# Expert routing rewritten: ranks row by row, counts and prefix on TensorE, the first two gathers issued inside the routing block

## The chip, the cores and the metric

The kernel runs on 1 core of one Trainium2 chip. The metric is device microseconds of one execution, the median of several. Lower is better.

## The reference, cut to what matters

A decoder layer on x (8, 256, 512): attention, then a long convolution with the context, then a mixture of experts, each on the layer-normalised x and added to it. The change is in the routing of the last one:

```python
logits = jnp.einsum('bsh,he->bse', x, Wr) + br          # 2048 tokens, E = 12 experts
probs = jax.nn.softmax(logits, axis=-1)
top_vals, top_idx = jax.lax.top_k(probs, K)             # K = 3
ew = jax.nn.softmax(top_vals, axis=-1)
for e in range(E):
    sel = top_idx == e
    mask = sel.any(axis=-1)
    cnt = sel.sum()
    w_e = jnp.sum(jnp.where(sel, ew, 0.0)) / jnp.maximum(cnt, 1)
    h = jax.nn.relu(jnp.einsum('bsh,hi->bsi', x, w1[e]) + b1[e])
    h = jnp.einsum('bsi,ih->bsh', h, w2[e]) + b2[e]
    out = out + mask[..., None] * (w_e * h)
```

An expert's weight w_e is one number for all its tokens. In `top_k` the lower index wins a tie.

## The kernel before, in words

The kernel is written for each engine by hand, in order, with semaphores. It has five blocks, one after the other: `attention`, `convolution`, `route`, `experts`, `finish`. At the end of a block all engines meet; the next block starts when the last has arrived.

`convolution` leaves the logits in `prob` (128 tokens on the partitions, NT = 16 token tiles, E = 12) and the normalised rows of x in DRAM, `xnd`.

`route` turns them into tables for `experts`. Tokens are sorted by expert into NTILE = 59 tiles of 128 places. `gidx` says which row of `xnd` a place gathers, `sidx` where its result is added, `wt` and `eid` are weight and expert of a tile, `tstart_i` is the first tile of an expert, `wexp` the weight of an expert. Almost all of it is one chain on VectorE (DVE); `do` means that the next instruction waits for this one. Its steps:

- softmax (L1193 to L1198), with an exp on ScalarE (ACT, L1147);
- rank of each expert of a token: all pairs are compared in one array of 16 x 12 x 12, greater (L1205), equal (L1206), equal and of a lower index (L1207), their sum (L1208), and the reduction over the rival (L1209); `sel` marks ranks under 3 (L1210);
- the softmax of the three best (L1212 to L1218), with a second exp on ACT;
- three fp32 matmuls (L1165 to L1167): places inside a token tile (`ps_c`), counts and weights by token tile (`ps_m`);
- a prefix sum over the 16 token tiles in five doubling steps (L1226 to L1231), the counts, the expert weights (L1236 to L1239);
- tiles by expert (L1242 to L1257), weight of each tile (L1258 to L1260), slot of each token and expert (L1262 to L1264), the slots of the three picks (L1266 to L1275);
- for each pick two one-hot tables in bf16, the place (16 x 128, L1286) and the tile with two values (16 x 59 each, L1284, L1288, L1289), that TensorE (PE) multiplies (L1174) into `ps_r`;
- `gidx` (L1300), `sidx` (L1304), the first expert's bias times its weight (L1306).

Beside it SP loads the weights of expert 0 in four quarters of 128 x 2560 (`w_lo`). ACT rounds each to fp32r (`upper`, L1151) and DVE takes the rest (`lower`, L1189), since a product is made of a high and a low part. ACT runs exp, `upper(0)`, exp, `upper(1)` to `upper(3)`. DVE runs `lower(0)` while it would wait for the counts and `lower(1)` while PE multiplies the last one-hot tables. `lower(2)` and `lower(3)` are the first work of DVE in `experts` (L1412), behind a wait for both copies of the gather indices (`gi_ready`, L1438).

`experts` starts with POOL (GpSimd): it copies an index column (L1438) and issues the indirect DMA that gathers 128 rows (`xg`, L1441), twice. PE transposes the first tile (`x_t`, L1564) when it has landed, ACT copies and rounds it (L1504, L1505), PE runs the first product (L1579, L1580 with `xh`, L1584 with `xl`, the low part that POOL makes, L1447), and from then on the tiles follow each other. The first product waits for the first two quarters of the weights, the second product (L1602) for all four. With all four split, SP starts to load the weights of expert 1, which DVE splits (L1405, L1407) and which must be there when the first tile of expert 1 comes; before each further expert DVE waits for PE (L1416).

Of the kernel before, what the change touches and what calls it, by code (L numbers as in the profile page):

```python
# [1081 lines left out]
def route(nc, cst, prob, w_hi, w_lo, split_done, wcat, b2, b2_sb, b2_in, b2_ready, tabs):  # L1082


    gidx, sidx, wt, eid, tstart_i, wexp = tabs
# [771 lines left out]
```

## Time and profile before

| | |
|---|---|
| median of 3 runs | 1593.04 us (1591.39 to 1593.26) |
| the profiled execution | 1590.1 us, its span 1588.1 us |
| PE busy | 1413.3 us (89%) |
| DVE busy | 792.1 us (50%) |
| POOL busy | 850.9 us (54%) |
| ACT busy | 679.8 us (43%) |
| granted TensorE clock, mean | 0.949 |

Times within the trace are in us from the start of the span. Busy shares are averages over five blocks with different limits; the routing block lies between about 545 and 601 us, where PE hardly works.

### The profile page before, as it was taken

What the parts mean: (1) busy time and instruction counts of PE and PEld (TensorE: products, weight loads), DVE (VectorE), ACT (ScalarE), POOL (GpSimd) and SP (SyncE); (2) the same over time, 40 slices, a digit from 0 to 9 for tenths busy, and PEclk for the clock granted to TensorE, in tenths of its full rate; (3) what the DMA queues carried; (4) which work ended last, traced back from release to release, by engine and by line L of the source; (5) the groups of instructions that cost most, each with busy time, mean ns of one, the idle gap of its engine ahead of it and who ended that gap; (6) DMA issues with size and microseconds to landing.
All of it is one profiled execution on the core that took longest, in us unless ns stands there. A gap on an engine that the chain in (4) does not pass through costs nothing. (4 is left out here: it accounts for less than half of the span.)

```text
span 1588.1 us, 27314 instructions
## 1 busy us (share of the span) xinstructions
PE 1413.3 (89%) x7642; PEld 1083.8 (68%) x7643; DVE 792.1 (50%) x1068; ACT 679.8 (43%) x1845; POOL 850.9 (54%) x990
## 2 busy tenths in 40 slices
PE   3899999669997417999999999999999999999956
PEld 1555555447775316888888888888888888888842
DVE  3456655548999698274434707446453552000003
ACT  0545546513444412444444444444444444444420
POOL 1444455134465204767666766767676766656530
PEclk9999999979999657999999999999999999999977
DMA  6000000034342514354444535444453542332115
GB/s 250 3 1 0 0 0 1 1 109 154 96 126 88 203 62 135 91 158 108 111 105 101 146 64 149 114 113 119 125 139 73 131 114 65 89 83 34 26 31 214
DMA packets 75461, 148.20 MB, mean 93 GB/s; under 512 B 9056, under 2 KB 13664, under 8 KB 74912
## 3 DMA queue, kind: packets, MB, share of 16 engines
q1 hardware_dynamic: 59424, 110.36, 22.3%
q0 software_dynamic: 14320, 35.40, 11.3%
q10 hardware_dynamic: 1680, 1.97, 0.4%
q8 instruction: 20, 0.33, 0.1%
q14 instruction: 17, 0.14, 0.0%
HBM read 115.11 MB, written 32.59 MB: 93 GB/s over the span
## 5 line engine op out<-in xcount | busy, mean ns | idle before, releaser
L1579 PE MATMUL ps_h<-w_hi,xh 128*128 x708 | 250.5, 365 | 1.5 <-ACT xh L1505 1.4
L1580 PE MATMUL ps_h<-w_lo,xh 128*128 x708 | 246.0, 359 | 0.0
L1602 PE MATMUL ps_y<-w_hi,hh 128*128 x590 | 239.9, 407 | 4.4 <-issue 4.4
L1407 DVE TENSOR_TENSOR w_lo<-stage,w_hi 128x512 f32 x220 | 223.9, 1018 | 27.0
L1603 PE MATMUL ps_y<-w_lo,hh 128*128 x590 | 233.8, 396 | 0.0
L1458 POOL TENSOR_TENSOR y<-y,b_sb 128x512 f32<-128x512 f32 x59 | 80.0, 1357 | 233.0 <-ACT y L1530 233.0
L1451 POOL TENSOR_TENSOR hl<-h,hh 128x1280 fp32r<-128x1280 f32 x59 | 190.9, 3235 | 13.1 <-ACT hh L1524 13.1
L933 PE MATMUL ps_b<-kv,toe 128*128 128x288 f32 x640 | 162.1, 414 | 12.9 <-DMA toe<-kpad 9.5
L1511 ACT ACTIVATE h<-ps_h 128x512 f32<-128x512 f32 x177 | 80.6, 528 | 212.8 <-POOL hl L1451 204.5
L1584 PE MATMUL ps_h<-w_hi,xl 128*128 x708 | 166.9, 357 | 0.0
L1520 ACT ACTIVATE h<-ps_td,b_now 128x128 f32<-128x128 f32 x590 | 158.6, 391 | 3.9 <-PE ps_td L1592 1.2
L1530 ACT ACTIVATE y<-ps_y,wt 128x512 f32<-128x512 f32 x59 | 40.7, 689 | 276.7 <-PE ps_y L1606 276.7
L933 PEld LDWEIGHTS ps_b<-kv,toe 128*128 128x128 f32 x640 | 123.0, 194 | 48.2 <-DMA toe<-kpad 10.4
L1579 PEld LDWEIGHTS ps_h<-w_hi,xh 128*128 128x128 f32 x708 | 133.4, 188 | 23.8 <-issue 2.1
L1580 PEld LDWEIGHTS ps_h<-w_lo,xh 128*128 128x128 f32 x708 | 133.7, 189 | 21.9
L1606 PE MATMUL ps_y<-w_hi,hl 128*128 x590 | 147.1, 395 | 0.0
L1405 DVE CAST w_hi<-stage 128x512 f32 x220 | 142.6, 648 | 5.7 <-DMA stage<-in_wcat 5.0
L1584 PEld LDWEIGHTS ps_h<-w_hi,xl 128*128 128x128 f32 x708 | 120.8, 188 | 21.8
L1602 PEld LDWEIGHTS ps_y<-w_hi,hh 128*128 128x128 f32 x590 | 111.8, 190 | 29.2 <-issue 4.6
L1416 DVE TENSOR_TENSOR turn<-wt 128x1 f32<-128x1 f32 x11 | 3.4, 312 | 253.4 <-PE ps_h L1584 253.4
L1606 PEld LDWEIGHTS ps_y<-w_hi,hl 128*128 128x128 f32 x590 | 110.5, 187 | 27.1
L1603 PEld LDWEIGHTS ps_y<-w_lo,hh 128*128 128x128 f32 x590 | 111.8, 190 | 24.3
(213 smaller groups left out, 2311.7 us busy)
## 6 DMA issues: line engine op xcount, KB each, us to landing
stage<-in_wcat SPq DMA_DIRECT2D x220, 256.0 KB
toe<-kpad SPq DMA_DIRECT2D x32, 256.0 KB, 3.3
cc<-in_ctx_rev SPq DMA_DIRECT2D x32, 192.0 KB, 3.4
w_lo<-in_wcat SPq DMA_DIRECT2D x4, 1280.0 KB, 11.8
acc<-added_c POOLq DMA_DIRECT2D x1, 4352.0 KB, 16.6
xs<-in_x SPq DMA_DIRECT2D x4, 1024.0 KB, 13.1
x2d<-xs SPq DMA_DIRECT2D x16, 256.0 KB, 2.5
xnd<-xn_c SPq DMA_DIRECT2D x16, 256.0 KB, 2.1
```

What stands on the lines that cost most here:

```text
L933: last = nc.tensor.matmul(view(ps[:], (4 * par + l) * 512, [[SPAN, B], [1, NPAIR]]), toe[:, par, (l - m) * P:(l - m + 1) * P], kv[:, buf, ...
L1405: nc.vector.tensor_copy(hi, stage[:, c % NSTAGE]).then_inc(w_rounded, 1)
L1407: nc.vector.tensor_tensor(lo, stage[:, c % NSTAGE], hi.bitcast(F32), ALU.subtract).then_inc(split_done, 1)
L1451: nc.gpsimd.tensor_tensor(hl[:], h[:], hh[:].bitcast(F32), ALU.subtract).then_inc(hl_ready, 1)
L1511: nc.scalar.activation(h[:, lo:hi], ps_h[:, c, 0:hi - lo], ACT.Copy).then_inc(h_evac, 1)
L1520: last = nc.scalar.activation(h[:, k * P:(k + 1) * P], ps_t[:, k // 4, (k % 4) * P:(k % 4 + 1) * P], ACT.Relu, bias=b1_now[:, k:k + 1])
L1579: nc.tensor.matmul(out, x_hi, part(w_hi, e, k * FF + lo, hi - lo), start=(k == 0), stop=False)
L1580: nc.tensor.matmul(out, x_hi, part(w_lo, e, k * FF + lo, hi - lo), start=False, stop=False)
L1584: last = nc.tensor.matmul(out, xl[:, k * P:(k + 1) * P], part(w_hi, e, k * FF + lo, hi - lo), start=False, stop=(k == KD - 1))
L1602: nc.tensor.matmul(ps_y[:], h_hi, part(w_hi, e, KD * FF + k * D, D), start=(k == 0), stop=False)
L1603: nc.tensor.matmul(ps_y[:], h_hi, part(w_lo, e, KD * FF + k * D, D), start=False, stop=False)
L1606: last = nc.tensor.matmul(ps_y[:], hl[:, k * P:(k + 1) * P], part(w_hi, e, KD * FF + k * D, D), start=False, stop=(k == KF - 1))
```

## The change

- Ranks: for each of the 12 experts its row is compared with the experts of lower index (>=) and with those of higher index (>), 22 instructions of 16 x 1 to 16 x 11 instead of four of 16 x 12 x 12. POOL clears the diagonal first. The reduction (L1237 of the changed kernel) stays.
- The largest probability is not searched again: it is the reciprocal of the softmax's sum, which is still in `den`. The subtraction for the second exp comes right behind the rank; `sel` is bf16 now.
- DVE sums `sel` and `ew` over the token tiles itself (`total`), so TensorE needs 12 columns for the counts and 12 for the weights. The places and the prefix over token tiles come from TensorE: 16 matmuls in bf16 that add up in `ps_c`. ACT makes the two bf16 matrices at the block's start, ahead of the first exp.
- `lower(0)` stands where `lower(1)` was; `lower(1)` stands behind `gidx`.
- The one-hot tables for tiles are 60 columns wide (59 used).
- POOL copies the first two index columns and issues the first two gathers inside `route`, as soon as `gidx` is there. The buffers `gi` and `xg` with their semaphores are made by the caller.
- The weights of the tiles and of the experts are made at the end, behind `lower(1)` and `sidx`.
- In `experts`, DVE waits for POOL's first `xl` instead of the index copies before it runs `lower(2)` and `lower(3)`.

```diff
--- before.py
+++ after.py
...
-def route(nc, cst, prob, w_hi, w_lo, split_done, wcat, b2, b2_sb, b2_in, b2_ready, tabs):
+def route(nc, cst, prob, w_hi, w_lo, split_done, wcat, b2, b2_sb, b2_in, b2_ready, xnd, first, tabs):
...
+    gi, xg, gi_ready, g_in = first
...
-        sel = sb("sel", [P, NT, E])
+        sel = sb("sel", [P, NT, E], BF16)
+        up_h = sb("up_h", [P, P], BF16)
+        one_h = sb("one_h", [P, P], BF16)
+        total = sb("total", [P, 2, E])
...
-        before = sb("before", [P, 2, NT + 1, E])
...
-        PLACE, TILE = NT * P, NT * NTILE
-        work = sb("work", [P, 2 * NT * E * E])
+        tile_f = sb("tile_f", [P, 4, NTILE])
+        COLS = NTILE + NTILE % 2
+        PLACE, TILE = NT * P, NT * COLS
+        work = sb("work", [P, max(NT * E * E, PLACE + 5 * TILE // 2)])
...
+            nc.scalar.activation(up_h[:], cst[:, C_UP:C_UP + P], ACT.Copy).then_inc(ones_ready, 1)
+            nc.scalar.activation(one_h[:], cst[:, C_ONE:C_ONE + P], ACT.Copy).then_inc(ones_ready, 1)
             exp(0)
             upper(0)
             exp(1)
             for q in range(1, NPART):
                 upper(q)
 
+        @block.gpsimd
+        def _(pool):
+            diag = view(work[:], 0, [[E * E, NT], [E + 1, E]])
+            nc.gpsimd.memset(diag, 0.0).then_inc(diag_zero, 1)
+            pool.wait_ge(gidx_ready, 1)
+            for i in range(2):
+                nc.gpsimd.tensor_copy(gi[:, i:i + 1], gidx[:, i:i + 1]).then_inc(gi_ready, 1)
+            pool.wait_ge(gi_ready, 2)
+            for i in range(2):
+                pool.indirect_dma_start(xg[:, i], None, xnd, bass.IndirectOffsetOnAxis(ap=gi[:, i:i + 1], axis=0))\
+                    .then_inc(g_in[i], 16)
+
         @block.tensor
         def _(pe):
 
+            ones = cst[:, C_ONE:C_ONE + P]
+            flat = sel[:].rearrange("p t e -> p (t e)")
+            pe.wait_ge(ones_ready, 2)
             pe.wait_ge(sel_ready, 1)
-            flat = sel[:].rearrange("p t e -> p (t e)")
-            nc.tensor.matmul(ps_c[:, 0:TE], cst[:, C_UP:C_UP + P], flat, start=True, stop=True)
-            nc.tensor.matmul(ps_m[:, 0:TE], cst[:, C_ONE:C_ONE + P], flat, start=True, stop=True)
-            nc.tensor.matmul(ps_m[:, TE:2 * TE], cst[:, C_ONE:C_ONE + P], ew[:].rearrange("p t e -> p (t e)"),
-                             start=True, stop=True).then_inc(counted, 1)
+            nc.tensor.matmul(ps_m[:, 0:E], ones, total[:, 0], start=True, stop=True).then_inc(counted, 1)
+            nc.tensor.matmul(ps_c[:, 0:TE], up_h[:], flat, start=True, stop=False)
+            for t in range(1, NT):
+                last = nc.tensor.matmul(ps_c[:, t * E:TE], one_h[:], flat[:, 0:TE - t * E], start=False,
+                                        stop=(t == NT - 1))
+            last.then_inc(placed, 1)
+            pe.wait_ge(ew_ready, 1)
+            nc.tensor.matmul(ps_w[:, 0:E], ones, total[:, 1], start=True, stop=True).then_inc(weighed, 1)
 
             for k in range(TOPK):
                 pe.wait_ge(hot_ready, k + 1)
                 oc, oa = place_hot(k), value_hot(k)
                 for t in range(NT):
-                    last = nc.tensor.matmul(ps_r[:, 0, 0:2 * NTILE], oc[:, t * P:(t + 1) * P],
-                                            oa[:, t * 2 * NTILE:(t + 1) * 2 * NTILE], start=(k == 0 and t == 0),
+                    last = nc.tensor.matmul(ps_r[:, 0, 0:2 * COLS], oc[:, t * P:(t + 1) * P],
+                                            oa[:, t * 2 * COLS:(t + 1) * 2 * COLS], start=(k == 0 and t == 0),
                                             stop=(k == TOPK - 1 and t == NT - 1))
                 last.then_inc(hot_used, 1)
...
-            gt = view(work[:], 0, [[E * E, NT], [E, E], [1, E]])
-            eq = view(work[:], NT * E * E, [[E * E, NT], [E, E], [1, E]])
-            other = view(prob[:], 0, [[E, NT], [0, E], [1, E]])
-            own = view(prob[:], 0, [[E, NT], [1, E], [0, E]])
-            low = view(cst[:], C_LOW, [[0, NT], [E, E], [1, E]])
-            v.tensor_tensor(gt, other, own, ALU.is_gt)
-            do(v.tensor_tensor(eq, other, own, ALU.is_equal))
-            do(v.tensor_tensor(eq, eq, low, ALU.mult))
-            do(v.tensor_tensor(gt, gt, eq, ALU.add))
-            do(v.tensor_reduce(rank[:], gt, AX_X, ALU.add))
+            dve.wait_ge(diag_zero, 1)
+            beats = view(work[:], 0, [[E * E, NT], [E, E], [1, E]])
+            for e in range(E):
+                own = view(prob[:], e, [[E, NT], [0, E - 1]])
+                for lo, hi, op in ((0, e, ALU.is_ge), (e + 1, E, ALU.is_gt)):
+                    if lo < hi:
+                        last = v.tensor_tensor(view(work[:], e * E + lo, [[E * E, NT], [1, hi - lo]]),
+                                               view(prob[:], lo, [[E, NT], [1, hi - lo]]),
+                                               view(prob[:], e, [[E, NT], [0, hi - lo]]), op)
+            do(last)
+            do(v.tensor_reduce(rank[:], beats, AX_X, ALU.add))
+            v.tensor_tensor(ex[:], prob[:], bc(den, E), ALU.subtract).then_inc(exp_in, 1)
             do(v.tensor_scalar(sel[:], rank[:], float(TOPK), None, ALU.is_lt))
-
-            do(v.tensor_reduce(mx, prob[:], AX_X, ALU.max))
-            v.tensor_tensor(ex[:], prob[:], bc(mx, E), ALU.subtract).then_inc(exp_in, 1)
+            v.tensor_reduce(total[:, 0], sel[:].rearrange("p t e -> p e t"), AX_X, ALU.add).then_inc(sel_ready, 1)
             dve.wait_ge(exp_out, 2)
-            do(v.tensor_tensor(ex[:], ex[:], sel[:], ALU.mult))
-            do(v.tensor_reduce(den, ex[:], AX_X, ALU.add))
-            do(v.reciprocal(den, den))
-            v.tensor_tensor(ew[:], ex[:], bc(den, E), ALU.mult).then_inc(sel_ready, 1)
-            v.memset(before[:, :, 0], 0.0)
+            do(v.scalar_tensor_tensor(ex[:], rank[:], float(TOPK), ex[:], ALU.is_lt, ALU.mult))
+            do(v.tensor_reduce(mx, ex[:], AX_X, ALU.add))
+            do(v.reciprocal(mx, mx))
+            do(v.tensor_tensor(ew[:], ex[:], bc(mx, E), ALU.mult))
+            v.tensor_reduce(total[:, 1], ew[:].rearrange("p t e -> p e t"), AX_X, ALU.add).then_inc(ew_ready, 1)
             v.tensor_copy(iota_h[:], cst[:, C_IOTA:C_IOTA + P])
-            lower(0)
             dve.wait_ge(counted, 1)
 
 
             count, inv, weight, ntile, tstart, tend = (wexp[:] if i == 2 else cnt[:, i] for i in range(6))
-            do(v.tensor_copy(before[:, 0, 1:], ps_m[:, 0:TE].rearrange("p (t e) -> p t e", e=E)))
-            step, par = 1, 0
-            while step <= NT:
-                if step > 1:
-                    v.tensor_copy(before[:, 1 - par, 1:step], before[:, par, 1:step])
-                do(v.tensor_tensor(before[:, 1 - par, step:], before[:, par, step:], before[:, par, 0:NT + 1 - step],
-                                   ALU.add))
-                step, par = 2 * step, 1 - par
-            upto = before[:, par]
-            do(v.tensor_copy(count, upto[:, NT]))
-            v.tensor_reduce(weight, view(ps_m[:], TE, [[1, E], [E, NT]]), AX_X, ALU.add)
-            do(v.tensor_scalar(inv, count, 1.0, None, ALU.max))
-            do(v.reciprocal(inv, inv))
-            do(v.tensor_tensor(weight, weight, inv, ALU.mult))
-
+            do(v.tensor_copy(count, ps_m[:, 0:E]))
...
+            v.tensor_scalar(inv, tstart, float(P), None, ALU.mult)
...
-            do(v.tensor_tensor(tile_e, view(cst[:], C_IOTA, [[0, NTILE], [1, E]]), bc(expert, E), ALU.is_equal))
-            do(v.tensor_tensor(tile_e, tile_e, view(weight, 0, [[0, NTILE], [1, E]]), ALU.mult))
-            do(v.tensor_reduce(wt[:], tile_e, AX_X, ALU.add))
-
-            do(v.tensor_tensor(slot[:], upto[:, 0:NT], ps_c[:, 0:TE].rearrange("p (t e) -> p t e", e=E), ALU.add))
-            do(v.tensor_scalar(inv, tstart, float(P), None, ALU.mult))
-            do(v.tensor_tensor(slot[:], slot[:], view(inv, 0, [[0, NT], [1, E]]), ALU.add))
+
+            dve.wait_ge(placed, 1)
+            do(v.tensor_tensor(slot[:], ps_c[:, 0:TE].rearrange("p (t e) -> p t e", e=E),
+                               view(inv, 0, [[0, NT], [1, E]]), ALU.add))
...
-                do(v.tensor_tensor(in_tile, view(iota_h[:], 0, [[0, NT], [1, NTILE]]),
-                                   bc(h_tile[:, k * NT:(k + 1) * NT], NTILE), ALU.is_equal))
+                do(v.tensor_tensor(in_tile, view(iota_h[:], 0, [[0, NT], [1, COLS]]),
+                                   bc(h_tile[:, k * NT:(k + 1) * NT], COLS), ALU.is_equal))
                 v.tensor_tensor(oc, view(iota_h[:], 0, [[0, NT], [1, P]]),
                                 bc(h_place[:, k * NT:(k + 1) * NT], P), ALU.is_equal)
                 v.tensor_scalar(oa[:, :, 0], in_tile, cst[:, C_TOK:C_TOK + 1], None, ALU.mult)
-                v.tensor_tensor(oa[:, :, 1], in_tile, bc(iota_h[:, 0:NT], NTILE), ALU.mult).then_inc(hot_ready, 1)
-            lower(1)
+                v.tensor_tensor(oa[:, :, 1], in_tile, bc(iota_h[:, 0:NT], COLS), ALU.mult).then_inc(hot_ready, 1)
+            lower(0)
...
+            m_place, m_tile = ps_r[:, 0, 0:NTILE], ps_r[:, 0, COLS:COLS + NTILE]
+            used, tok, to = (tile_f[:, i] for i in range(1, 4))
...
-            v.tensor_copy(gidx[:], tok)
-            do(v.tensor_scalar(expert, tok, trash, None, ALU.subtract))
-            do(v.tensor_tensor(expert, expert, used, ALU.mult))
-            do(v.tensor_scalar(expert, expert, trash, None, ALU.add))
-            v.tensor_copy(sidx[:], expert)
+            v.tensor_copy(gidx[:], tok).then_inc(gidx_ready, 1)
+            dve.wait_ge(gi_ready, 2)
+            lower(1)
+            do(v.tensor_scalar(to, tok, trash, None, ALU.subtract))
+            do(v.tensor_tensor(to, to, used, ALU.mult))
+            do(v.tensor_scalar(to, to, trash, None, ALU.add))
+            v.tensor_copy(sidx[:], to)
+
+            dve.wait_ge(weighed, 1)
+            v.tensor_copy(weight, ps_w[:, 0:E])
+            do(v.tensor_scalar(inv, count, 1.0, None, ALU.max))
+            do(v.reciprocal(inv, inv))
+            do(v.tensor_tensor(weight, weight, inv, ALU.mult))
+            tile_w = view(work[:], 0, [[E, NTILE], [1, E]])
+            do(v.tensor_tensor(tile_w, view(cst[:], C_IOTA, [[0, NTILE], [1, E]]), bc(expert, E), ALU.is_equal))
+            do(v.tensor_tensor(tile_w, tile_w, view(weight, 0, [[0, NTILE], [1, E]]), ALU.mult))
+            do(v.tensor_reduce(wt[:], tile_w, AX_X, ALU.add))
             dve.wait_ge(b2_in, 16)
             v.tensor_scalar(b2_sb[:, 0], b2_sb[:, 0], wexp[:, 0:1], None, ALU.mult).then_inc(b2_ready, 1)
...
+    gi, xg, gi_ready, g_in = first
...
-        gi = sb("gi", [P, 2], U32)
...
-        xg = sb("xg", [P, 2, D])
...
-            dve.wait_ge(gi_ready, 2)
+            dve.wait_ge(xl_ready, 2)
...
-            gather(0, 0)
-            gather(1, 1)
...
+                    first = (right("gi", [P, 2], U32), right("xg", [P, 2, D]), busy.enter_context(nc.semaphore("gi_ready")),
+                             [busy.enter_context(nc.semaphore(f"g_in{i}")) for i in range(2)])
```

The order of the ranks on DVE. Before (`work` holds all pairs, `rank` the result):

```order
L1198 TENSOR_TENSOR prob<-ex,col 128x192
L1205 TENSOR_TENSOR work<-prob 128x2304
L1206 TENSOR_TENSOR work<-prob 128x2304
L1207 TENSOR_TENSOR work<-work,cst 128x2304
L1208 TENSOR_TENSOR work<-work 128x2304
L1209 TENSOR_REDUCE rank<-work 128x192
L1210 TENSOR_SCALAR sel<-rank 128x192
L1212 TENSOR_REDUCE col<-prob 128x16
L1213 TENSOR_TENSOR ex<-prob,col 128x192
```

and of the change, the first and the last of the 22 comparisons with what follows:

```order
L1225 TENSOR_TENSOR prob<-ex,col 128x192
L1233 TENSOR_TENSOR work<-prob 128x16x11
...
L1233 TENSOR_TENSOR work<-prob 128x16x11
L1237 TENSOR_REDUCE rank<-work 128x192
L1238 TENSOR_TENSOR ex<-prob,col 128x192
L1239 TENSOR_SCALAR sel<-rank 128x192
L1240 TENSOR_REDUCE total<-sel 128x12
L1242 SCALAR_TENSOR_TENSOR ex<-rank,ex 128x192
```

The four large operations became 22 small ones, and the input of the second exp (`ex`) is made before `sel`.

The end of the routing on DVE, from `gidx` on. Before:

```order
L1300 CAST gidx<-tile_f 128x59
L1301 TENSOR_SCALAR tile_f<-tile_f,cst 128x59
L1302 TENSOR_TENSOR tile_f<-tile_f 128x59
L1303 TENSOR_SCALAR tile_f<-tile_f,cst 128x59
L1304 CAST sidx<-tile_f 128x59
L1306 TENSOR_SCALAR b_sb<-b_sb,wexp 128x512
```

and of the change:

```order
L1310 CAST gidx<-tile_f 128x59
L1216 TENSOR_TENSOR w_lo<-w_lo,w_hi 128x2560
L1313 TENSOR_SCALAR tile_f<-tile_f,cst 128x59
L1314 TENSOR_TENSOR tile_f<-tile_f 128x59
L1315 TENSOR_SCALAR tile_f<-tile_f,cst 128x59
L1316 CAST sidx<-tile_f 128x59
L1319 COPY wexp<-ps_w 128x12
L1320 TENSOR_SCALAR cnt<-cnt 128x12
L1321 RECIPROCAL cnt<-cnt 128x12
L1322 TENSOR_TENSOR wexp<-wexp,cnt 128x12
L1324 TENSOR_TENSOR work<-cst,tile_f 128x708
L1325 TENSOR_TENSOR work<-work,wexp 128x708
```

A quarter of the weights (`w_lo`) and the weights of experts and tiles now stand between `gidx` and the end of the block.

POOL, at the border of `route` and `experts`. Before, all of it in `experts`:

```order
L1427 UNCONDITIONAL_BRANCH
L1438 COPY gi<-gidx 128x1
L1435 TENSOR_TENSOR tick<-wt 128x1
L1441 DMA xg<-xnd,gi 128x512
L1438 COPY gi<-gidx 128x1
L1435 TENSOR_TENSOR tick<-wt 128x1
L1441 DMA xg<-xnd,gi 128x512
L1447 TENSOR_TENSOR xl<-xf,xh 128x512
```

and of the change, where the two branches after the gathers are the way into `experts`:

```order
L1169 UNCONDITIONAL_BRANCH
L1172 MEMSET work 128x16x12
L1175 COPY gi<-gidx 128x1 x2
L1178 DMA xg<-xnd,gi 128x512 x2
L1087 UNCONDITIONAL_BRANCH
L1447 UNCONDITIONAL_BRANCH
L1467 TENSOR_TENSOR xl<-xf,xh 128x512
```

Copies and gathers moved in front of the block's end.

## Rows read from the trace of the kernel before

**Rows 1.** Busy time of each engine by stretch (start:end, length, engines, clock, DMA share, GB/s).

```profile
566.00:602.00 36.00, 5.49 (x49) 4.53 (x48) 33.58 (x67) 3.10 (x2) 0.25 (x2) 0.50 0.00 0
640.00:740.00 100.00, 100.00 (x519) 83.92 (x518) 43.69 (x55) 45.59 (x113) 69.84 (x79) 1.00 0.44 108
```

**Rows 2.** Timeline of PE (start, length, operation, idle before it and its releaser).

```profile
606.03 1.12 PE L1564 MATMUL ps_xd<-cst,xg 128*128 128x128 f32 x4 [8.11 <-DMA xg<-xnd,gi]
608.60 0.79 PE L1579 MATMUL ps_h<-w_hi,xh 128*128 x1 [1.44 <-ACT xh L1505]
```

**Rows 3.** Timeline of DVE, the comparisons of the ranks.

```profile
548.15 2.56 DVE L1205 TENSOR_TENSOR work<-prob 128x2304 f32<-128x2304 f32 x1
550.62 2.55 DVE L1206 TENSOR_TENSOR work<-prob 128x2304 f32<-128x2304 f32 x1
...
558.39 2.55 DVE L1209 TENSOR_REDUCE rank<-work 128x192 f32<-128x2304 f32 x1
```

**Rows 4.** Timeline of ACT in the routing: the first quarter rounded, the second exp.

```profile
554.18 2.34 ACT L1151 ACTIVATE w_hi<-w_lo 128x2560 fp32r<-128x2560 f32 x1 [7.13 <-DMA w_lo<-in_wcat]
562.06 0.36 ACT L1147 ACTIVATE ex<-ex 128x192 f32<-128x192 f32 x1 [5.54 <-DVE ex L1213]
```

**Rows 5.** Timeline of DVE, second softmax, first quarter, prefix, weights, slots.

```profile
562.45 0.36 DVE L1215 TENSOR_TENSOR ex<-ex,sel 128x192 f32<-128x192 f32 x1 [0.43 <-ACT ex L1147]
...
563.94 2.82 DVE L1189 TENSOR_TENSOR w_lo<-w_lo,w_hi 128x2560 fp32r<-128x2560 f32 x1
566.68 0.35 DVE L1226 COPY before<-ps_m 128x192 f32<-128x192 f32 x1
...
570.28 0.17 DVE L1242 TENSOR_SCALAR cnt<-cnt 128x12 f32<-128x12 f32 x1
...
574.40 0.88 DVE L1258 TENSOR_TENSOR work<-cst,tile_f 128x708 f32<-128x708 f32 x1
...
577.17 0.35 DVE L1262 TENSOR_TENSOR slot<-before,ps_c 128x192 f32<-128x192 f32 x1
...
578.16 0.36 DVE L1266 SCALAR_TENSOR_TENSOR ex<-rank,slot 128x192 f32<-128x192 f32 x1
```

**Rows 6.** Timeline of DVE, the one-hot tables and the second quarter.

```profile
581.35 1.14 DVE L1284 TENSOR_TENSOR work<-iota_h,slot_h 128x944 bf16<-128x944 bf16 x1
582.53 2.29 DVE L1286 TENSOR_TENSOR work<-iota_h,slot_h 128x2048 bf16<-128x2048 bf16 x1
...
596.03 2.82 DVE L1189 TENSOR_TENSOR w_lo<-w_lo,w_hi 128x2560 fp32r<-128x2560 f32 x1
```

**Rows 7.** Timeline of DVE, the end of the routing and the start of the experts.

```profile
599.62 0.19 DVE L1300 CAST gidx<-tile_f 128x59 uint32<-128x59 f32 x1
...
600.65 0.48 DVE L1306 TENSOR_SCALAR b_sb<-b_sb,wexp 128x512 f32<-128x512 f32 x1
603.95 5.58 DVE L1412 TENSOR_TENSOR w_lo<-w_lo,w_hi 128x2560 fp32r<-128x2560 f32 x2 [2.82 <-POOL gi L1438]
```

**Rows 8.** Timeline of POOL from the start of the experts.

```profile
601.67 0.18 POOL L1438 COPY gi<-gidx 128x1 uint32<-128x1 uint32 x1 [61.82 <-POOLq L1086]
...
604.27 3.40 POOL L1441 DMA_INDIRECT xg<-xnd,gi  x1
608.35 2.32 POOL L1447 TENSOR_TENSOR xl<-xf,xh 128x512 fp32r<-128x512 f32 x1 [0.68 <-ACT xh L1505]
```

**Rows 9.** The line of the gathers: length of one in ns (min/median/max), and time to landing.

```profile
L1441 POOL DMA_INDIRECT xg<-xnd,gi x59: 992/1037/3400, 602.5 to 1482.3; - x59
...
DMA to landing us min/median/max: 3.3/3.8/6.4
```

**Rows 10.** Timeline of DVE, its first wait for PE before an expert's weights.

```profile
673.55 0.16 DVE L1416 TENSOR_TENSOR turn<-wt 128x1 f32<-128x1 f32 x1 [27.09 <-PE ps_h L1584]
```

**Rows 11.** Busy time by stretch at the start of the experts.

```profile
608.00:613.00 5.00, 4.41 (x11) 3.50 (x12) 3.11 (x3) 0.27 (x1) 3.63 (x4) 0.52 0.60 182
613.00:618.00 5.00, 5.00 (x31) 4.29 (x29) 3.71 (x8) 1.42 (x3) 0.00 (x0) 1.00 0.70 240
```

More of the change, by code:

```diff
@@ L1115, in route @@
         ps_m = psum("ps_m", [P, 512])
+        ps_w = psum("ps_w", [P, 512])
         ps_r = psum("ps_r2", [P, 1, 512])
@@ L1118, in route @@
         exp_in, exp_out = sem("exp_in"), sem("exp_out")
-        sel_ready, counted = sem("sel_ready"), sem("counted")
+        ones_ready, sel_ready, counted, placed = sem("ones_ready"), sem("sel_ready"), sem("counted"), sem("placed")
+        ew_ready, weighed = sem("ew_ready"), sem("weighed")
+        diag_zero, gidx_ready, step_g = sem("diag_zero"), sem("gidx_ready"), sem("step_g")
         hot_ready, hot_used = sem("hot_ready"), sem("hot_used")
@@ L1248, in _ @@
             v.tensor_copy(tstart_i[:], tstart[0:1])
+            v.tensor_scalar(inv, tstart, float(P), None, ALU.mult)
             do(v.tensor_tensor(tend, tstart, ntile, ALU.add))
             tile_e = view(work[:], 0, [[E, NTILE], [1, E]])
-            expert, is_e, first = tile_f[:, 0], tile_f[:, 1], tile_f[:, 2]
+            expert = tile_f[:, 0]
             do(v.tensor_tensor(tile_e, view(cst[:], C_IOTA, [[1, NTILE], [0, E]]), view(tend, 0, [[0, NTILE], [1, E]]),
@@ L1288, in _ @@
                 v.tensor_scalar(oa[:, :, 0], in_tile, cst[:, C_TOK:C_TOK + 1], None, ALU.mult)
-                v.tensor_tensor(oa[:, :, 1], in_tile, bc(iota_h[:, 0:NT], NTILE), ALU.mult).then_inc(hot_ready, 1)
-            lower(1)
+                v.tensor_tensor(oa[:, :, 1], in_tile, bc(iota_h[:, 0:NT], COLS), ALU.mult).then_inc(hot_ready, 1)
+            lower(0)
             dve.wait_ge(hot_used, TOPK)
-            m_place, m_tile = ps_r[:, 0, 0:NTILE], ps_r[:, 0, NTILE:2 * NTILE]
-            used, tok = is_e, first
+            m_place, m_tile = ps_r[:, 0, 0:NTILE], ps_r[:, 0, COLS:COLS + NTILE]
+            used, tok, to = (tile_f[:, i] for i in range(1, 4))
             trash = cst[:, C_TRASH:C_TRASH + 1]
@@ L1309, in experts @@
 def experts(nc, cst, w_hi, w_lo, stage, stage_in, split_done, wcat, b2, b2_sb, b2_in, b2_ready, b1_sb, xnd, x2d, x2,
-            x2_in, acc, tabs):
+            x2_in, acc, first, tabs):
     gidx, sidx, wt, eid, tstart_i, wexp = tabs
+    gi, xg, gi_ready, g_in = first
     with ExitStack() as ctx:
@@ L1344, in experts @@
         CHUNKS = [(0, 512), (512, 1024), (1024, FF)]
-        gi_ready, si_ready = sem("gi_ready"), sem("si_ready")
-        g_in = [sem("g_in0"), sem("g_in1")]
+        si_ready = sem("si_ready")
         x_done = sem("x_done")
@@ L1795, in decoder_layer @@
                     b2_ready = busy.enter_context(nc.semaphore("b2_ready"))
+                    first = (right("gi", [P, 2], U32), right("xg", [P, 2, D]), busy.enter_context(nc.semaphore("gi_ready")),
+                             [busy.enter_context(nc.semaphore(f"g_in{i}")) for i in range(2)])
                     route(nc, cst, prob, w_hi, w_lo, split_done, a["wcat"], a["L0_ffn_b2"], b2_sb,
-                          b2_in, b2_ready, tabs)
+                          b2_in, b2_ready, xnd, first, tabs)
                     experts(nc, cst, w_hi, w_lo, stage, stage_in, split_done, a["wcat"], a["L0_ffn_b2"], b2_sb, b2_in,
-                            b2_ready, b1_sb, xnd, x2d, x2, x2_in, acc, tabs)
+                            b2_ready, b1_sb, xnd, x2d, x2, x2_in, acc, first, tabs)
                 finish(nc, cst, x2, x2_in, acc, a["L0_ffn_Wp1"], a["L0_ffn_bp1"], a["L0_ffn_Wp2"], a["L0_ffn_bp2"], out)
```

1 line of the change is left out of this document (removed).

## The prediction, made before the changed kernel ran

> **What bounds the kernel now.** I read the busy time by stretch first. Between 640 and 740 us PE is busy all the time at full clock, and it stays so until the last tiles; between 566 and 602 it is busy for 5.5 us of 36 while DVE is for 33.6 [rows 1]. So the experts are bound by PE and the routing by DVE. The timeline of PE shows the border: the first transposition starts at 606.03, released by the landing of the gather, and the first product at 608.60 [rows 2]. From there PE is hardly idle. Whatever brings 608.60 forward comes off the whole time one to one, if nothing new holds PE afterwards. So I follow the DVE chain through the routing, then the way from its end to the first product.
>
> **The chain on DVE up to gidx.** Prices first. The same kind of operation takes 2.56 us for 2304 elements [rows 3] and about 0.88 for 708 [rows 5]: about 1.04 ns an element and a fixed part near 0.16. Started without a wait the next one begins 2.47 after the first (548.15 to 550.62), which is 0.07 over its elements; with a wait, 944 elements take 1.18 to the next start (581.35 to 582.53 [rows 6]), 0.20 over them.
>
> (a) Ranks. Removed: 548.15 to 558.39, 10.24 us [rows 3]. Added: 22 comparisons of 16 x 1 to 16 x 11, 2 x 16 x 66 = 2112 elements, 2.2 us, and 22 fixed parts. Only the last is waited for, so I take 0.07 each, 1.5 us: 3.7 in all. The ends are 2.2 (no fixed part) and 22 x 0.20 + 2.2 = 6.6 (each as if waited for). The reduction (2.55, and a few hundredths to the next start) then starts at 551.9 instead of 558.39 and the rank is there at 554.5. POOL's clearing of the diagonal starts with the block, two microseconds ahead of its use, and costs nothing.
>
> (b) The second exp does not keep up. ex is ready at 554.5 + 0.36 = 554.9. But ACT has upper(0) before exp(1) in its order, and upper(0) starts at 554.18, when its quarter has landed, and takes 2.34 [rows 4]. So exp starts at 556.5, and DVE goes on 0.4 behind that, as before (562.06 to 562.45 [rows 4, 5]), at 556.9 instead of 562.45. DVE, done with sel and total at about 555.4, has waited 1.5 us by then: **-5.6** for (a) and (b). This also caps (a): up to 1.5 us of extra cost in the ranks is hidden by that wait, beyond it it counts. The two bf16 copies that ACT makes lie before its first exp, while DVE makes that one's input; they may cost 0 to 0.3, I take 0.
>
> (c) From there to the old start of lower(0), 1.49 us before (562.45 to 563.94 [rows 5]); now one reduction more (0.27) and a wait: **+0.3**.
>
> (d) lower(0) leaves this place, 563.94 to 566.68 [rows 5]: **-2.7**. It takes the place of lower(1) at 596.03 [rows 6], with the same length and the same cover for PE's last product. What lower(0) covered, the wait for the counts, is short now: one matmul of 12 columns, 3 us ahead of its use.
>
> (e) Prefix, counts, expert weights: 566.68 to 570.28 [rows 5], 3.6 us, become one copy of 0.2: **-3.4**. The 16 prefix matmuls are needed some 6 us after their input; the three 192-column fp32 ones before fit in the 2.8 us of lower(0). Hidden.
>
> (f) Tile weights leave: 574.40 to 577.17 [rows 5], **-2.8**.
>
> (g) Slots: 577.17 to 578.16 becomes one operation of 0.39 and one unwaited one of 0.08: **-0.5**.
>
> (h) One-hot tables: 581.35 to 596.03 [rows 6], 14.7 us. 60 instead of 59 columns add 16 elements to each of nine operations, 0.15 us, and the tensor_scalar may gain as much: 0. The 2048-element comparison in bf16 takes 2.29, one element a cycle like fp32 [rows 6], although its rows are of even width: one operand repeats one value along the row, as in the tile tables.
>
> Sum: gidx starts **14.7** earlier, at 584.9 instead of 599.62 [rows 7].
>
> **From gidx to the first product.** (i) DVE now waits for POOL's two copies (0.18 each [rows 8]) with a semaphore each way: +0.6; bounds 0.4 and 2.8, what DVE waited for the copies at 603.95 when an issue lay between them [rows 7]. Then lower(1) +2.7, expert weights +0.8, tile weights +2.7. The routing ends on DVE at 601.13 (600.65 + 0.48 [rows 7]) - 14.7 + 6.8 = 593.2, that is **-7.9**.
>
> (j) Before, 4.90 us passed from DVE's end to the first transposition: 0.54 to the first instruction of POOL (601.67 [rows 8]), then copy, issue, landing. Now the gather is issued at about 585.9. It takes 3.8 us to land in the median and 6.4 at most [rows 9], so it is there by 592.3, before the block ends. What is left is the entry into the block: 0.54 is the nearest row; I take 0.6 for PE, between 0.5 and 2.0, since PE's own entry is hidden behind the gather in this trace. **-4.3**. The steps from there to the first product (2.57 us [rows 2]) stay.
>
> (k) lower(2) and lower(3), 5.6 us [rows 7], now start behind xl, about 6 us later against the product. The second product that needs them comes 18 us after the first. Expert 1's weights are also loaded 6 us later against PE; DVE had 27.1 us to spare before the next expert [rows 10]. Price 0 unless that cover is gone. In exchange xl is no longer slowed by them; it was not waited for.
>
> (l) The clock: 0.52 of full between 608 and 613, 1.00 after [rows 11], so it rose about 4 us behind the first product. I take the same; a rise at once gives 2 us (half of 4), one that comes twice as late costs 2.
>
> **Sum:** -7.9 - 4.3 = **-12.2 us**. The profiled execution took 1590.1, which gives 1577.9. It lies 2.9 under the median of the runs (1593.04), so for the median I say **1580.8**. The unknowns (a, at most +1.4 beyond the cover; i and j, -0.3 to +3.6; l, 2 either way; not all at once) make this case's own range 1578 to 1584.5.
>
> A rule against the change: the Trainium skill (VectorE: DVE Perf Modes, The TRN2 errata) says small instructions pay a fixed cost each, (N + 151) cycles at 0.96 GHz for an fp32 tensor_tensor. By it the 22 comparisons would be an estimated 5.7 us, 2.0 more than I take, 0.5 beyond the cover, and the time 1581.3; the length of a single operation agrees [rows 3], but the start of the next one does not wait for it.
>
> **Rivals.**
> 1. *The entry replaces the gather.* PE has its own first instructions to do in the block and nothing in the trace shows their length; if the start of the block is as long as the old wait, (j) gives nothing: 1585.1. For: POOL is the only engine seen entering there. Against: it needed 0.54 only [rows 8]. 8%.
> 2. *DVE holds up POOL.* The issue that ran beside lower(2) took 3.40 against 1.04 in the median [rows 8, 9], and xl 2.32. Now both issues stand beside lower(1) and the tile weights. Two of 3.4 end at 592.9, just inside; if the second lasts until DVE is done and then takes its 1.0, the block ends 1 to 2 us late: 1582 to 1583. 8%. The Trainium skill (GPSIMD Engine Reference, 8. Key points) says that GpSimd contends with Vector instructions of two SBUF inputs; the rows agree.
> 3. *The even width pays.* If the tile tables ran at two elements a cycle, six operations of 1.14 would save half a microsecond each: 1577.9. Against: the 128-wide one does not [rows 6]. 3%. The Trainium skill (VectorE: DVE Perf Modes, What auto-detection actually checks) asks for 16-bit operands of step 1, which the repeated operand is not.
> 4. *Slower: the clock stays low.* PE idles longer between the last one-hot product and the transposition (about 10.5 us against 8.1 [rows 2]). If TensorE then stayed at 1.2 GHz, each microsecond costs half of one. To lose the 12.2 and come out 3.2 slower it would have to stay low for about 31 us longer than the 4 us of now. Against: once PE was busy without a gap it rose at once [rows 11]. 1.5%, 1597 or more.
>
> **How the numbers follow.** The forecast has 78%, the rivals 8, 8, 3 and 1.5; 1.5 remain for a loss that just cancels the gain. 0.2% is 3.2 us, about what a measurement of this kernel can tell from no change. Faster by more than that (under 1589.9) are all but the last two: 0.97; 0.015 and 0.015 for the rest. The range from 1577.5 to 1585.5 holds the first case, rival 1, 2 and 3.
>
> **What would show it.** Right: the rank's reduction starts about 3.7 us after prob; DVE then waits about 1.5 us for ACT's exp behind upper(0); no rows of the prefix on DVE; gidx near 585; POOL's gathers in the routing, the first longer than 1.04; the first transposition near 594 with no DMA in front, and the first product near 596.4; the second expert's first wait of DVE still over 15 us. Wrong: comparisons that each cost 0.2 over their elements; a transposition that waits for the gather or for the entry; a clock that rises much later; any PE wait for weights behind the first tiles.

## The result, and the profile after

| | before | after |
|---|---|---|
| median | 1592.65 us (4 runs, 1591.39 to 1593.26) | 1563.72 us (4 runs, 1563.44 to 1566.66) |
| ratio | | 0.9824, 95% interval 0.9807 to 0.9841 |
| profiled execution | 1590.1 us, span 1588.1 | 1563.66 us, span 1561.5 |
| routing's first DVE instruction to first product | 62.70 us | 50.94 us |
| first product to first matmul of `finish` | 940.6 us | 924.05 us |

28.9 us came off, where 12.2 were forecast; the range ended at 1577.5. The last two rows of the table say where: the forecast is about the first, and that one fell by 11.8. Another 16.6 us came off the experts, where the forecast had put nothing. Both are differences between the starts of instructions: 545.90 (DVE, L1193) to 608.60 [rows 2] to 1549.24 before

```profile
1549.24 9.80 PE L1705 MATMUL ps_pool<-o_sb,cst 128*4 128x512 f32 x16 [14.22 <-DMA o_sb<-acc]
```

and in the timeline of the changed kernel (DVE and PE):

```profile
548.38 0.35 DVE L1220 TENSOR_REDUCE col<-prob 128x16 f32<-128x192 f32 x1 [0.56 <-PEq L660]
...
596.78 1.09 PE L1582 MATMUL ps_xd<-cst,xg 128*128 128x128 f32 x4 [10.79 <-ACTq L1515]
599.32 0.79 PE L1597 MATMUL ps_h<-w_hi,xh 128*128 x1 [1.44 <-ACT xh L1523]
...
1523.37 6.90 PE L1723 MATMUL ps_pool<-o_sb,cst 128*4 128x512 f32 x11 [14.28 <-DMA o_sb<-acc]
```

The first transposition waits for no DMA any more. The routing began 2.5 us later in this execution than in the one of before; over all runs of this study it began between 545.8 and 550.1, in old and new kernels alike, so this is the variation of the blocks ahead of it.

The routing itself, DVE's timeline of the changed kernel, against [rows 3, 5, 6, 7]:

```profile
550.61 3.82 DVE L1233 TENSOR_TENSOR work<-prob 128x176 f32<-128x176 f32 x22
554.47 2.55 DVE L1237 TENSOR_REDUCE rank<-work 128x192 f32<-128x2304 f32 x1
557.06 0.36 DVE L1238 TENSOR_TENSOR ex<-prob,col 128x192 f32<-128x192 f32 x1
557.33 0.25 DVE L1239 TENSOR_SCALAR sel<-rank 128x192 bf16<-128x192 f32 x1
557.62 0.51 DVE L1240 TENSOR_REDUCE total<-sel 128x12 f32<-128x192 bf16 x1
559.33 0.36 DVE L1242 SCALAR_TENSOR_TENSOR ex<-rank,ex 128x192 f32<-128x192 f32 x1 [1.20 <-ACT ex L1154]
...
561.33 0.16 DVE L1252 COPY cnt<-ps_m 128x12 f32<-128x12 f32 x1
561.52 0.17 DVE L1254 TENSOR_SCALAR cnt<-cnt 128x12 f32<-128x12 f32 x1
...
569.29 1.16 DVE L1294 TENSOR_TENSOR work<-iota_h,slot_h 128x960 bf16<-128x960 bf16 x1
...
584.07 2.82 DVE L1216 TENSOR_TENSOR w_lo<-w_lo,w_hi 128x2560 fp32r<-128x2560 f32 x1
...
587.66 0.19 DVE L1310 CAST gidx<-tile_f 128x59 uint32<-128x59 f32 x1
588.31 2.83 DVE L1216 TENSOR_TENSOR w_lo<-w_lo,w_hi 128x2560 fp32r<-128x2560 f32 x1 [0.46 <-POOL gi L1175]
...
595.51 0.49 DVE L1328 TENSOR_SCALAR b_sb<-b_sb,wexp 128x512 f32<-128x512 f32 x1
```

22 comparisons in 3.86 us; a new wait of 1.20 for ACT's exp; one-hot tables of the same 14.8 us; gidx 39.28 us after the first instruction instead of 53.72.

The experts. The busy time by stretch has 500 us of PE at 100% and full clock in both kernels. First the kernel before, then the changed one (columns as in [rows 1]):

```profile
740.00:1240.00 500.00, 500.00 (x2574) 418.83 (x2573) 245.51 (x316) 230.63 (x576) 339.18 (x384) 1.00 0.46 115
```

```profile
740.00:1240.00 500.00, 500.00 (x2614) 424.69 (x2613) 253.19 (x324) 236.92 (x594) 352.09 (x395) 1.00 0.47 117
```

Same clock, same busy share, but 1.6% more matmuls. The transpositions of x, one group per tile, give the period of a tile. Before, 15.54 us, then after, 15.28:

```profile
704.44 0.60 PE L1564 MATMUL ps_xd<-cst,xg 128*128 128x128 f32 x4
719.98 0.60 PE L1564 MATMUL ps_xd<-cst,xg 128*128 128x128 f32 x4
```

```profile
708.49 0.60 PE L1582 MATMUL ps_xd<-cst,xg 128*128 128x128 f32 x4
723.77 0.60 PE L1582 MATMUL ps_xd<-cst,xg 128*128 128x128 f32 x4
```

Over 48 tiles the period is 15.540 and 15.287 us. 0.253 us times 59 tiles is 14.9 of the 16.6. All instructions of a tile are the same in both kernels. What the diff does change there is one thing that I had read past: `gi` (8 bytes per partition) and `xg` (4096) left the left side of SBUF, and all buffers behind them moved down. In the built programs xh, xl, hh and hl, the stationary operands of the products (the ones that PE loads ahead of a matmul), start at a multiple of 64 bytes before and 32 beyond one after; the weights, the moving operands that stream through, start 32 beyond one in both.

### The profile page after: what moved, and what is told of

Read it like the earlier page. It is cut to its first block and busy times, and to the rows that moved or that the text cites. A ratio compares the mean times of both kernels' runs of the same rounds, so it can differ in the third digit from the quotient of the medians.

```text
span 1561.5 us, 27353 instructions
## 1 busy us (share of the span) xinstructions
PE 1396.8 (89%) x7656; PEld 1080.8 (69%) x7657; DVE 783.9 (50%) x1075; ACT 680.7 (44%) x1847; POOL 862.8 (55%) x989
## 5 line engine op out<-in xcount | busy, mean ns | idle before, releaser
L1427 DVE TENSOR_TENSOR w_lo<-stage,w_hi 128x512 f32 x220 | 236.3, 1074 | 27.0
L1597 PE MATMUL ps_h<-w_hi,xh 128*128 x708 | 247.1, 361 | 1.5 <-ACT xh L1523 1.4
L1598 PE MATMUL ps_h<-w_lo,xh 128*128 x708 | 242.2, 354 | 0.0
L1425 DVE CAST w_hi<-stage 128x512 f32 x220 | 134.3, 610 | 6.5 <-DMA stage<-in_wcat 6.0
## 6 DMA issues: line engine op xcount, KB each, us to landing
xs<-in_x SPq DMA_DIRECT2D x4, 1024.0 KB, 13.7
```

Of the source, the lines that this page charges most:

```text
L1425: nc.vector.tensor_copy(hi, stage[:, c % NSTAGE]).then_inc(w_rounded, 1)
L1427: nc.vector.tensor_tensor(lo, stage[:, c % NSTAGE], hi.bitcast(F32), ALU.subtract).then_inc(split_done, 1)
L1597: nc.tensor.matmul(out, x_hi, part(w_hi, e, k * FF + lo, hi - lo), start=(k == 0), stop=False)
L1598: nc.tensor.matmul(out, x_hi, part(w_lo, e, k * FF + lo, hi - lo), start=False, stop=False)
```

## The experiments

The first six move buffers by unused bytes and leave every instruction as it is.

**The old kernel with 32 bytes ahead of the experts' buffers.**

```diff
+        pad = sb("pad", [P, 8])
         gi = sb("gi", [P, 2], U32)
```

> The kernel before, with one unused buffer of 32 bytes per partition ahead of the first buffer of the experts block, so that all buffers there (xh, xl, hh, hl, which PE loads as stationary operands, among them) start 32 bytes later: at 32 beyond a multiple of 64, as in the changed kernel, instead of at a multiple of 64. The routing is the old one. Theory A (the start address of the buffers that PE loads decides how far apart matmuls start): tile period 15.54 -> about 15.29 us, time about 1592.7 - 15 = 1577.5. Theory B (the experts block got faster through what the change does in the routing, or through the 4 KB of xg that left the left side): no change, 1592.7, period 15.54.

Measured 1576.87 us (1575.8 to 1579.02, ratio to before 0.9898, interval 0.9881 to 0.9914), period 15.287:

```profile
706.89 0.60 PE L1565 MATMUL ps_xd<-cst,xg 128*128 128x128 f32 x4
722.18 0.60 PE L1565 MATMUL ps_xd<-cst,xg 128*128 128x128 f32 x4
```

The routing is the old one (62.79 us to the first product), and 15.9 us are gone. Theory B falls: neither the routing nor the 4 KB of xg, which are still on the left here, made the experts faster.

**The same with 64 bytes.**

```diff
+        pad = sb("pad", [P, 16])
         gi = sb("gi", [P, 2], U32)
```

> The kernel before with 64 unused bytes in the same place: all buffers of the experts block move, but stay at multiples of 64. Theory A: no change, 1592.7 and a period of 15.54. Rival A2 (not the alignment, but any move of the buffers against each other or against the weights changes it): some other period than 15.54.

1591.21 us (1590.08 to 1594.79, ratio 0.9994, interval 0.9984 to 1.0003), period 15.533. Moving alone does nothing.

**The changed kernel with 32 bytes**, so that its buffers start at multiples of 64 again.

```diff
+        pad = sb("pad", [P, 8])
         si = sb("si", [P, 2], U32)
```

> The changed kernel with 32 unused bytes ahead of the buffers of the experts block, so that they start at multiples of 64 again. Theory A: the period goes back to about 15.54 and the time to about 1563.7 + 15 = 1579; what is left of the gain, some 12 to 14 us, is the routing's. Theory B: 1563.7, period 15.29.

1579.07 us (1577.41 to 1579.59, ratio 0.9906), period 15.540:

```profile
711.14 0.60 PE L1583 MATMUL ps_xd<-cst,xg 128*128 128x128 f32 x4
726.68 0.60 PE L1583 MATMUL ps_xd<-cst,xg 128*128 128x128 f32 x4
```

This is the change without its side effect: 13.7 us faster than before by the medians, 11.6 by the stretch of the routing (51.14 against 62.70). Of the 2 us between them 1.2 lie in the clock of the last tile, see (l) below.

**The changed kernel with the weights moved by 32 bytes instead.**

```diff
+                pad_r = late.enter_context(nc.sbuf_tensor("pad_r", [P, 8], F32, side="right"))
                 w_hi = late.enter_context(nc.sbuf_tensor("w_hi", [P, 2, WS], F32R, side="right"))
```

> The changed kernel with 32 unused bytes beyond the weights, so that w_hi and w_lo (the moving operands) start at a multiple of 64 and xh, xl, hh, hl stay at 32 beyond one. Theory A1 (the stationary operand's own start decides): period 15.29, 1563.7. Theory A3 (stationary and moving operand must start alike within 64 bytes): period about 15.54, time about 1579. If the moving operand's own start at a multiple of 64 is good by itself, the period falls under 15.29.

1578.08 us (1577.06 to 1579.29, ratio 0.9906), period 15.540:

```profile
708.81 0.60 PE L1582 MATMUL ps_xd<-cst,xg 128*128 128x128 f32 x4
724.35 0.60 PE L1582 MATMUL ps_xd<-cst,xg 128*128 128x128 f32 x4
```

The stationary operands are where the fast kernel has them, and it is slow. It is not their own start that counts. The buffers behind the weights on that side (`stage`, `xg`, `gi`) move by 32 bytes too, but do not explain it: `xg` starts 32 beyond a multiple of 64 in the fast first experiment as well, and all of them start in the next run, which is fast, where they start here.

**Both moved**, weights and stationary operands at multiples of 64.

```diff
+        pad = sb("pad", [P, 8])
         si = sb("si", [P, 2], U32)
...
+                pad_r = late.enter_context(nc.sbuf_tensor("pad_r", [P, 8], F32, side="right"))
                 w_hi = late.enter_context(nc.sbuf_tensor("w_hi", [P, 2, WS], F32R, side="right"))
```

> The changed kernel with both moves: the weights start at a multiple of 64 and so do xh, xl, hh, hl. Stationary and moving operand start alike again, at 0 instead of at 32. Theory A3 (alike within 64 bytes is what counts): period 15.29, time 1563.7. Theory A4 (each operand costs by itself when it starts at a multiple of 64, and only 32 beyond is good): a period of 15.54 or more, 1579 or more.

1565.89 us (1565.64 to 1568.08, ratio 0.9839, interval 0.9824 to 0.9854), period 15.283:

```profile
709.66 0.60 PE L1583 MATMUL ps_xd<-cst,xg 128*128 128x128 f32 x4
724.95 0.60 PE L1583 MATMUL ps_xd<-cst,xg 128*128 128x128 f32 x4
```

Fast again, at other addresses: theory A3 holds and A4 falls.

**Only the operands of the second product moved**, the changed kernel with the 32 bytes between xl and h. Behind them h, hh, hl and y move.

```diff
         xl = sb("xl", [P, KD * P], F32R)
+        pad = sb("pad", [P, 8])
         h = sb("h", [P, FF])
```

> The changed kernel with 32 unused bytes between xl and h: xh and xl still start like the weights (32 beyond a multiple of 64), hh and hl, the stationary operands of the second product, no longer do. Theory A3 for each matmul by itself: the 30 matmuls of the second product lie about 233 ns apart again, those of the first product stay at about 229, the period becomes 15.29 + 30 x 0.0045 = 15.42, the time 1563.7 + 8 = 1571.5. Rival (the whole block changes its pace by something else that moves with the buffers): 15.29 or 15.54.

1571.44 us (1570.52 to 1571.98, ratio 0.9868), period 15.411. The groups by line show it product by product. The changed kernel, first the `xl` matmuls of the first product, then the `hl` ones of the second (between the bars busy us and mean ns of one, behind them the idle time ahead):

```profile
L1602 PE MATMUL ps_h<-w_hi,xl 128*128 x708 | 164.1, 354 | 0.0
L1624 PE MATMUL ps_y<-w_hi,hl 128*128 x590 | 144.9, 392 | 0.0
```

this kernel:

```profile
L1603 PE MATMUL ps_h<-w_hi,xl 128*128 x708 | 164.7, 355 | 0.0
L1625 PE MATMUL ps_y<-w_hi,hl 128*128 x590 | 147.1, 395 | 0.0
```

and the changed one with all of them moved (the third experiment):

```profile
L1603 PE MATMUL ps_h<-w_hi,xl 128*128 x708 | 167.5, 358 | 0.0
L1625 PE MATMUL ps_y<-w_hi,hl 128*128 x590 | 147.1, 395 | 0.0
```

The first product keeps its pace (355), the second has the slow one (395). So the price is paid in the product whose own operands start unlike, and not by the block as a whole.

The other runs take the routing apart, on the changed kernel.

**The first two gathers back in the experts block.**

```diff
-            pool.wait_ge(gidx_ready, 1)
-            for i in range(2):
-                nc.gpsimd.tensor_copy(gi[:, i:i + 1], gidx[:, i:i + 1]).then_inc(gi_ready, 1)
-            pool.wait_ge(gi_ready, 2)
-            for i in range(2):
-                pool.indirect_dma_start(xg[:, i], None, xnd, bass.IndirectOffsetOnAxis(ap=gi[:, i:i + 1], axis=0))\
-                    .then_inc(g_in[i], 16)
...
-            dve.wait_ge(gi_ready, 2)
             lower(1)
...
+            gather(0, 0)
+            gather(1, 1)
             x_lo(0)
```

> The changed kernel with the first two gathers (index copies and indirect DMAs) back at the start of the experts block; all buffers and the rest of the routing as changed. Theory: the landing of the first gather is on the path again, 1.27 -> about 5.4 us from the routing's last DVE instruction to the first transposition, and DVE is spared 0.5 us of waiting for the index copies: first product 3.6 us later, about 1567.3. Rival (the block's entry alone costs as much, or the reordering of DVE's work did it): less than 1 us.

1568.70 us (1567.83 to 1571.25), 5.0 over the changed kernel by the medians and 3.3 by the stretch from the routing to the first product (54.26 against 50.94), where 3.6 were expected; the other 1.7 us are not placed. The timeline at the border:

```profile
594.98 0.49 DVE L1320 TENSOR_SCALAR b_sb<-b_sb,wexp 128x512 f32<-128x512 f32 x1
596.00 0.18 POOL L1450 COPY gi<-gidx 128x1 uint32<-128x1 uint32 x1 [47.00 <-POOLq L1087]
...
600.30 1.11 PE L1576 MATMUL ps_xd<-cst,xg 128*128 128x128 f32 x4 [14.30 <-DMA xg<-xnd,gi]
```

From DVE's end (595.47) to the transposition 4.83 us, as before the change; the landing is on the path again.

**The second exp ahead of the first rounding.**

```diff
             exp(0)
-            upper(0)
             exp(1)
+            upper(0)
```

> The changed kernel with ACT's second exp ahead of the rounding of the first quarter of the weights. Theory: DVE's 1.20 us wait for that exp goes, everything behind it comes 1.2 us sooner, about 1562.5; the rounding of the first quarter comes 0 to 1 us later and is still 20 us ahead of its use. Rival (something else is late there, such as the counts from TensorE): no gain.

1561.32 us (1560.36 to 1564.98), 1.1 less in the traces (49.84 against 50.94). DVE's wait is gone:

```profile
555.10 0.50 DVE L1240 TENSOR_REDUCE total<-sel 128x12 f32<-128x192 bf16 x1
555.51 0.35 DVE L1242 SCALAR_TENSOR_TENSOR ex<-rank,ex 128x192 f32<-128x192 f32 x1
```

**The old comparisons.** The four large instructions of the kernel before in place of the 22, the rest as changed.

```diff
-            beats = view(work[:], 0, [[E * E, NT], [E, E], [1, E]])
-            for e in range(E):
...
-            do(v.tensor_reduce(rank[:], beats, AX_X, ALU.add))
+            gt = view(work[:], 0, [[E * E, NT], [E, E], [1, E]])
...
+            v.tensor_tensor(gt, other, own, ALU.is_gt)
+            do(v.tensor_tensor(eq, other, own, ALU.is_equal))
+            do(v.tensor_tensor(eq, eq, low, ALU.mult))
+            do(v.tensor_tensor(gt, gt, eq, ALU.add))
+            do(v.tensor_reduce(rank[:], gt, AX_X, ALU.add))
```

> The changed kernel with the four large comparisons of the old one for the ranks (and without the cleared diagonal). They take 10.2 us instead of 3.86, but the 1.2 us that DVE waits for the second exp go: theory 5.2 us slower, about 1568.9. If the wait behind the rounding did not cover anything, it would be 6.4.

1568.81 us (1567.1 to 1570.01), 5.1 slower; 5.2 in the traces (56.16). With the ranks late, DVE found the exp ready. The wait behind the rounding had hidden 1.2 of the 6.4 us that the small comparisons save.

**The changed kernel and the one with the early exp, side by side.**

> The changed kernel as it is, on the same chip as the next one: 1563.7.

> The changed kernel with ACT's second exp ahead of the first rounding, once more, beside the changed kernel on the same chip: 1.1 us faster by the stretch from routing to first product in the traces (49.83 against 50.94), 1562.6. If the 2.4 us between the medians of the first look were real, 1561.3.

1563.42 us (5 runs, 1563.15 to 1565.65; ratio to before 0.9823, interval 0.981 to 0.9837) and 1561.10 us (5 runs, 1559.15 to 1567.09; 0.9812, interval 0.9793 to 0.9831). The intervals overlap. The traces have 51.15 and 49.85 us for the stretch that the edit touches, so I take 1.1 to 1.3 us as its worth, and this kernel as the best of the study; the medians alone would not carry that.

## Why the prediction was wrong, point by point

What failed is a term that was put at nothing without a reason: the pace of the tiles. Behind "Whatever brings 608.60 forward comes off the whole time one to one" the sum has nothing for the experts but (k) and (l), both at 0. I took the block for unchanged because its instructions are, and did not follow where its buffers went. The missing term is 14.9 us by the period of the tiles; the run that gives it alone measured 15.9. The order of the instructions and the trace of before could not have priced it. But that two buffers of 8 and 4096 bytes leave from ahead of the stationary operands of the bound engine stands in the diff (in the built programs these operands move by 4128 bytes, not a multiple of 64), and a bound of either sign for it would have been due.

The kernel without that effect (1579.07) lies 1.7 under the forecast of 1580.8 and inside its own range. That it lies under it is luck: its stretch from the routing to the first product fell by 11.6, less than the 12.2 of the sum, and the clock of the last tile gave 1.2 that the sum had not seen. The steps of the sum, in the changed kernel:

- **(a) Ranks.** Forecast 3.7 for 2112 elements in 22 instructions, measured 3.86: the price of 0.07 us for an instruction that nobody waits for holds down to 16 elements (0.10 us from start to start; 0.26 with 176). The Trainium skill's formula (VectorE: DVE Perf Modes, The TRN2 errata) gave an estimated 5.7; no run here shows it for a chain without waits.
- **(b) ACT's order.** DVE resumed 10.95 us after its first instruction instead of 16.55, -5.6 as forecast. The wait was 1.20 instead of 1.5, since summing sel took 0.51. The early-exp run showed the wait real and the old comparisons showed its cover.
- **(c)** +0.5 instead of +0.3, for the second such sum. **(e)** 0.19, as forecast. **(h)** 14.78 against 14.68: the wider tables bring nothing, rival 3 is out. gidx -14.4 instead of -14.7.
- **(i)** The wait for the index copies cost 0.46; DVE's end came 8.34 after gidx, +6.8 against before, as forecast.
- **(j)** From DVE's end at 596.00 to the transposition 0.78 us, forecast 0.6: -4.1 instead of -4.3. Rival 1 is out. Rival 2's mechanism is there and its price is not. POOL's timeline, the two gathers:

```profile
588.51 3.64 POOL L1178 DMA_INDIRECT xg<-xnd,gi  x1 [0.29 <-POOL gi L1175]
592.46 0.95 POOL L1178 DMA_INDIRECT xg<-xnd,gi  x1 [0.31 <-issue]
```

  and what the trace says of that line's landings:

```profile
DMA to landing us min/median/max: 3.5/4.8/6.1
```

  The first issue lasted 3.64 us beside lower(1), and landed after 6.1 at most, 594.6. The second took 0.95 us beside the tile weights, and POOL was done at 593.4. PE began at 596.78, so 2.2 us of cover are left. The Trainium skill's rule (GPSIMD Engine Reference, 8. Key points), contention with DVE instructions of two SBUF inputs, fits the first issue and xl, which took 1.27 instead of 2.32 [rows 8] with DVE idle. The second issue does not show it: it was as short as one alone, though a comparison of 708 elements with two such inputs (L1324, 592.73 to 593.63) ran beside it.
- **(k)** DVE had 18.6 us to spare at the first wait, where it was 27.1 [rows 10]:

```profile
662.83 0.25 DVE L1436 TENSOR_TENSOR turn<-wt 128x1 f32<-128x1 f32 x1 [18.61 <-PE ps_h L1602]
```

  The cover held, at two thirds of its size.
- **(l)** In this execution the clock rose sooner, not later (busy time by stretch, the granted clock third from the end):

```profile
599.00:602.00 3.00, 2.68 (x6) 2.15 (x7) 1.54 (x1) 0.00 (x0) 2.84 (x3) 0.50 0.00 0
602.00:607.00 5.00, 5.00 (x25) 4.16 (x24) 4.08 (x3) 1.03 (x2) 4.74 (x2) 0.96 0.00 0
```

  That is some 3 us behind the first product instead of 4, worth half a microsecond. It is not the change: in the second trace of the same kernel (`e10_after_again`) the first product started at 597.29, and the clock was back only some 5.7 us behind it:

```profile
597.00:602.00 5.00, 4.71 (x11) 3.75 (x12) 3.58 (x2) 0.00 (x0) 4.72 (x4) 0.50 0.01 3
602.00:607.00 5.00, 5.00 (x27) 4.26 (x27) 2.05 (x2) 1.20 (x2) 2.85 (x1) 0.90 0.34 96
```

  Over all traces of this study it was 3.0 to 6.0 us. Rival 4, the slower one, needed 31 us more and is out. With 14.9 for the period and 0.5 here, about 1.2 us of the experts' 16.6 are left. They lie in the last tile, for which the sum had no term. There PE is idle for 4.35 us ahead of the second product, the clock falls to its lower level, 1.2 GHz, and comes back during the product. The kernel before (product from 1525.12), then the changed one (from 1500.58):

```profile
1525.00:1530.00 5.00, 4.88 (x12) 3.82 (x13) 0.00 (x0) 0.00 (x0) 2.99 (x2) 0.50 0.36 50
1500.50:1505.50 5.00, 4.92 (x16) 3.98 (x16) 0.00 (x0) 0.00 (x0) 2.94 (x2) 0.69 0.31 49
```

  The 20 matmuls with `hh` took 7.40 us before and 6.07 after. This too is hardly the change: they took 7.28 in the old kernel with 64 bytes, but 6.00 in the one with 32, which has the old routing.

## What to carry to other kernels

An edit that moves a buffer out of a block changes the start of everything allocated behind it: list the start addresses of the operands of the bound engine before and after, modulo 64 bytes, before the block is called unchanged. Where one chain on one engine sets the pace of a stage, take from it, in this order, what another engine can do, what can stand behind the point that others wait for (here gidx), and what waits only because of the order on a third engine (here the exp). Small instructions were dear when each waited for the one before (0.20 us over their elements), and not when only the last was waited for (0.07).
